# One stream for all attention tiles and feed-forward rounds of a six-layer block

## What is computed

```python
for i in range(6):
    x = attn_layer(shift_tokens(x), Wqkv[i], q_scale[i], k_scale[i], Wo[i]) + x
    x = ffn_layer(shift_tokens(x), ln_g[i], ln_b[i], W1[i], b1[i], W2[i], b2[i]) + x

def attn_layer(x, Wqkv, qs, ksc, Wo):        # 16 heads of 64
    q, k, v = split(x @ Wqkv)                # 128 -> 3 * 1024
    q = q / max(norm(q), 1e-12) * qs         # the floor under the norms
    k = k / max(norm(k), 1e-12) * ksc
    q, k = rotary(q), rotary(k)              # two products and a sum each
    out = local_attention(q, k, v)           # windows of 32, softmax
    return out @ Wo                          # 1024 -> 128

def ffn_layer(x, g, bln, W1, b1, W2, b2):
    xn = (x - mean) / sqrt(var + 1e-05) * g + bln
    a, gate = split(xn @ W1 + b1)            # 128 -> 2 * 341
    return a * gelu(gate) @ W2 + b2          # 341 -> 128
```

## Time and profile before

| | us |
|---|---|
| median of 3 runs | 4562.96 |
| lowest, highest | 4555.24, 4566.67 |
| the profiled execution | 4562.57 |
| its span on the core | 4560.5 |

### The profile page before, as it was taken

One profiled execution on the slowest core, in us unless ns is written; L12 is line 12 of the kernel. 1 busy time (PEld: TensorE's weight loads), 2 busy tenths in 40 slices (PEclk: granted clock), 3 DMA queues, 4 the chain that ended last, 5 costly groups with the idle time before them and its releaser, 6 DMA issues.

```text
span 4560.5 us, 148424 instructions
## 1 busy us (share of the span) xinstructions
PE 4214.2 (92%) x51751; PEld 2907.5 (64%) x51751; DVE 3501.8 (77%) x7368; ACT 2547.9 (56%) x5842; POOL 2884.7 (63%) x3664
## 2 busy tenths in 40 slices
PE   6999998999899988999889998999889998788899
PEld 4777775666666666666656666666666665566655
DVE  4666668997699967999679985999769995577566
ACT  2555555666466655666456663666546664355322
POOL 2333337887288855888378882888648885655300
PEclk9999999999999999999999998999999999887699
DMA  2000010000100010000100001000000000000000
GB/s 83 7 7 7 6 41 6 5 5 6 43 6 5 5 30 20 5 5 6 36 11 5 5 6 43 6 5 5 28 22 5 5 7 11 21 12 12 4 7 11
DMA packets 160438, 64.07 MB, mean 14 GB/s; under 512 B 121365, under 2 KB 155937, under 8 KB 159521
## 3 DMA queue, kind: packets, MB, share of 16 engines
q1 hardware_dynamic: 160288, 62.05, 5.3%
HBM read 26.54 MB, written 2.10 MB: 6 GB/s over the span
## 4 chain that ended last, share of the span: by engine, by line
PE 33%; DVE 29%; issue 25%; POOL 5%; ACT 4%; DVEq 1%; SPq 1%; ACTq 1%; POOLq 0%; DMA 0%
DVE ss L993 6%; DVE big L988 6%; DVE mx L1005 5%; PE pj L1535 3%; DVE big L987 3%; DVE e L1012 3%; DVE qn L987 3%; PE pj L1378 3%; PE turn L1454 3%; PE pp L1336 2%; PE sc L1547 2%; ACT big L698 2%; PE po L1351 2%; PE sc L1697 1%; PE turn L1535 1%
## 5 line engine op out<-in xcount | busy, mean ns | idle before, releaser
L1436 PE MATMUL pj<-wqkv,xcT 128*128 128x512 f32 x1536 | 830.4, 624 | 24.5 <-DVE big L988 9.6
L690 ACT ACTIVATE big<-pj 128x512 f32<-128x512 f32 x768 | 459.1, 598 | 244.3 <-PE pj L1436 176.1
L530 POOL TENSOR_TENSOR big<-big 128x512 f32<-128x512 f32 x384 | 486.0, 1277 | 132.0 <-DVE big L988 132.0
L988 DVE TENSOR_TENSOR big<-pj,ropes 128x512 f32<-128x512 f32 x768 | 522.4, 680 | 0.0
L530 POOL TENSOR_TENSOR qn<-qn,big 128x512 f32<-128x512 f32 x384 | 486.5, 1278 | 35.6 <-DVE big L988 35.6
L993 DVE TENSOR_REDUCE ss<-big 128x8 f32<-128x512 f32 x768 | 504.2, 678 | 0.1
L1524 PEld LDWEIGHTS pp<-wo,oT 128*128 128x128 f32 x3072 | 366.8, 196 | 154.5 <-ACT oT L713 154.1
L525 POOL TENSOR_TENSOR e<-e,rc 128x512 f32<-128x512 f32 x384 | 392.8, 1045 | 46.1 <-DVE rc L1023 46.1
L1524 PE MATMUL pp<-wo,oT 128*128 128x128 f32 x3072 | 403.9, 286 | 7.0 <-ACT oT L713 7.0
L519 POOL TENSOR_TENSOR qn<-qn,ny 128x512 f32<-128x512 f32 x384 | 396.9, 1045 | 7.5
L519 POOL TENSOR_TENSOR big<-big,ny 128x512 f32<-128x512 f32 x384 | 396.8, 1045 | 7.5
(11 more groups left out here) (322 smaller groups left out, 9605.8 us busy)
## 6 DMA issues: line engine op xcount, KB each, us to landing
wqkv<-in_L_ffn_Wqkv SPq DMA_DIRECT2D x6, 1536.0 KB, 6.5
xsd<-Y SPq DMA_DIRECT2D x192, 32.0 KB
xsd<-Y SPq DMA_DIRECT2D x384, 15.8 KB
xsf<-Y SPq DMA_DIRECT2D x96, 64.0 KB
xsf<-Y SPq DMA_DIRECT2D x192, 31.5 KB
xsx<-Y SPq DMA_DIRECT2D x64, 64.0 KB, 1.8
xsx<-CT SPq DMA_DIRECT2D x64, 64.0 KB, 1.9
wo<-in_L_ffn_Wo SPq DMA_DIRECT2D x6, 512.0 KB, 7.5
```

Of the source, the lines that this page charges most:

```text
L530: nc.gpsimd.tensor_tensor(U[a.par][i], U[a.par][i], t2b[i % 2], ALU.add).then_inc(sem("d_add"), 1)
L690: nc.scalar.activation(sqb[i % 2], pj[i % 2][:, :], ACT.Square).then_inc(sem("d_sq"), 1)
L988: nc.vector.tensor_tensor(t2v, swapped, sin, ALU.mult).then_inc(sem("d_r"), 1)
L1436: mm(pj[i % 2][:, :], xcT[:, a.par, :], wqkv[:, i * 512:i * 512 + 512], start=True, stop=True).then_inc(sem("d_ch"), 1)
```

## The change

The two phases of a layer and the six layers are one loop now. A `Pass` holds four tiles (stages `n`, `a`, `b`, `c`, as before) and five rounds (`rounds[0]` to `rounds[4]`, one stage each), and there is a pass for each of the 192 tiles and eight to drain. A round stage runs in every second pass: `hidden`, `gelu` and `gated` in the even ones (`even_round(3)`), statistics, normalisation and transposition (`odd_round(2)`) and the down projection with its residual sum (`odd_round(3)`) in the odd ones. Rounds trail the tiles by so much that their two tiles are finished. `all_layers` writes the first eight passes and the last eight out, and loops over the others: the eight passes at the seam of two layers once, the 24 inside a layer as six iterations of four.

What moves with it:

- `hidden` writes to `po[0]`, `po[1]`, `po[0]`, the banks of `pv`, and the GELU writes to a buffer of its own, `f_hidden`; `f_xcT` takes the place of `kT` as its input. The down projection writes to `pp` (before: `sc`) and the transpositions to `pt_` (before: `pp`).
- PE begins a pass with `chunk(0)` and not with `turn(0)`, and `turn` uses the banks `pt_` and `pp` in turn.
- ACT loads the GELU tables at the start of every even pass and the other set in the middle of it.
- On POOL `turn_sum(3)` stands ahead of the four small operations and of `unit(a, 0)`; `unit` and `probs` alternate.
- The weights are loaded in parts, each when its last reader is done: `wqkv` in three parts, `wo`, the norm, the up and the down weights. The eleven feed-forward loads stand between loads of tiles in SP's list.
- In the last layer the product with the gate, the sum into `X`, its statistics and its normalisation are spread over two passes, and the normalisation is on DVE (one `tensor_scalar` a tile) and not on POOL.
- `clamp` stays on DVE, ahead of `rope(3)`.

The core of the diff:

```diff
-        f_hid = [pj[0], pj[1], pt_]
+        f_hid = [po[0], po[1], po[0]]
+        f_hidden = sb("f_hidden", [P, 3, FT * P])
+        f_xcT = sb("f_xcT", [P, 2, FT * P])
...
+        LAGS, ROUND_LAGS, SEAM = 4, 5, 8
...
+        def all_layers(eng, body):
+            tiles, rounds = DEPTH * NT, DEPTH * NF
+            def known(k, **more):
...
+                body(Pass([one(k - i, tiles, NT) for i in range(LAGS)], [one(k // 2 - i, rounds, NF) for i in range(ROUND_LAGS)],
+                          k % 2, in_po=min(max(k - 3, 0), tiles), **more))
...
+            for k in range(SEAM):
+                known(k, at=k, layer=0)
+            with eng.Fori(0, DEPTH - 1) as l:
+                inside(l, False)
+                for p in range(SEAM):
+                    moving(l, NT + p, 0, at=p, layer=l + 1)
+            inside(DEPTH - 1, True)
+            for k in range(tiles, tiles + SEAM):
+                known(k, last=True)
...
+                if part == "q":
+                    past(sp, "d_ch", l * (4 * NT) - 2)
+                    sp.dma_start(wqkv[:, 0:INNER], Wqkv[l, :, 0:INNER]).then_inc(sem("wq_in"), 16)
...
+                unit(b, 1)
+                probs(0)
+                unit(b, 2)
+                probs(1)
+                unit(b, 3)
...
+                turn_sum(0)
+                mean_square(p.odd_round(2))
...
+                turn_sum(1)
+                inverse_deviation(p.odd_round(2))
...
+                turn_sum(2)
+                turn_sum(3)
...
+                if r:
+                    nc.scalar.preload_act_table_set("gelu_and_others")
+                square(0)
+                turned(0)
+                gelu(0)
...
+                if r or p.begins(0):
+                    nc.scalar.preload_act_table_set("natural_log_exp_and_others")
...
+                if p.begins(1):
+                    dve.wait_ge(sem("wq_in"), p.layer * 48 + 48)
...
+                rope(0)
+                square_sum(0)
+                gated(0)
+                rope(1)
+                if x:
+                    dve.wait_ge(sem("f_in%d" % x.par), x.half * 48 + 48)
+                    for i in range(FT):
+                        last = nc.vector.bn_stats(st[:, i, :], xsf[:, x.par, i, :])
...
+                clamp()
+                rope(3)
+                if x:
+                    past(dve, "f_rstd", x.g + 1)
+                    for i in range(FT):
+                        last = nc.vector.tensor_scalar(fxn[:, 128 * i:128 * i + 128], xsf[:, x.par, i, :], dif[:, 2 * i:2 * i + 1], rstd[:, i:i + 1], ALU.subtract, ALU.mult)
+                    last.then_inc(sem("f_xn"), 1)
+                if y:
+                    nc.vector.tensor_tensor(Y[:, ds, :], pp[:, 0:2 * D].rearrange("p (a d) -> p a d", a=2), Y[:, ds, :], ALU.add).then_inc(sem("y_ready"), FT)
                 row_max(0)
...
-                        for j in range(4):
-                            last = nc.tensor.transpose(pt_[:, j * P:j * P + P], U[b.par][i][:, j * P:j * P + P], ident)
+                        bank = (pt_, pp)[i % 2]
+                        for j in range(4):
+                            last = nc.tensor.transpose(bank[:, j * P:j * P + P], U[b.par][i][:, j * P:j * P + P], ident)
...
+                chunk(0)
+                hidden(0)
                 turn(0)
-                chunk(0)
                 turn(1)
                 chunk(1)
+                hidden(1)
```

More of the change, by code:

```diff
@@ L683, in _, with step @@
             stream(act, NT, x_body, 0, 0, 4)
[L685 removed]
+            def step(p):
+                n, a, b, c = p.n, p.a, p.b, p.c
+                r = p.even_round(3)
                 def square(i):
@@ L1121, in l_body @@
+            all_layers(dve, step)
             def l_body(a, b, c, d, e_, f):
@@ L1431, in chunk @@
                             past(pe, "d_xc", a.g + 1)
+                        if p.begins(1) and i % 2 == 0:
+                            pe.wait_ge(sem(("wq_in", "wk_in")[i // 2]), p.layer * (48, 32)[i // 2] + (48, 32)[i // 2])
                         if i < 2:
```

513 lines of the change are left out of this document (292 added, 221 removed).

## The result

| | us |
|---|---|
| kernel before, median (all its runs beside the changed one) | 4561.01 (4555.24 to 4566.67) |
| changed kernel, median | 4457.58 (4454.3 to 4462.36) |
| ratio | 0.9774, 95% interval 0.9757 to 0.9791 |
| profiled execution of the changed kernel; its span | 4454.3; 4452.4 |

The change makes the kernel 2.3% faster; 4441 was forecast. The spans of the two profiled executions differ by 108.1 us: 90.5 in the stretch of the layers, 15.2 in the last step (628.2 to 613.0 from its first transposition to the end), 2.4 ahead of the layers.

What follows compares the result with a forecast made beforehand. PE full and the loop through DVE closed bound a pass; filling and draining cost 40 us a layer. Pairs at 31.7 us, seams and ends gave 3113 us for the layers, 121 less: 4441 us, range 4345 to 4555.

Runs made afterwards that it cites:

- two_both: Changed kernel with two passes in its inner loop, the layers written out and all rotary tables worked out before the first layer; 4333.63 us, ratio 0.9497 to the kernel before.

## What to carry to other kernels

Count the instructions of a loop's body on its fullest engine before making it longer, and look at the instruction queue's packets and for idle time put down to "issue" at the loop's turn: here a body of four passes instead of two gave away 76 us of a possible 179. Where between 856 and 1699 instructions the edge lies, and what besides length sets it, these runs do not say. When phases are merged, write down the loop through each engine, POOL's too, because whichever order is changed for one waits in another. For a small DVE operation with both operands in SBUF, beside a busy POOL, the moment at which it starts sets its price: the same clamp costs 0.19, 0.77 or 1.04 us.

## What had not been expected of the hardware

- A turn of a loop whose 1699 PE instructions are read again costs 3.6 us of the stream, and 3.6 with twice the body (36.4 / 10); with 856 instructions it costs nothing. PE stands 2.0 to 2.4 us, and where its clock falls behind that, the turn costs 4.7 us and not 3.2.
- The same body in its second copy was read again at two of five turns only.
- Code that is run straight through cost nothing that could be seen: the five written-out seams of `two_both` add 1.4 us each, at 120 packets.
- An operand addressed through a register in the eight rotary products of a pass cost 0.12 us a pair.
- 0.6 us more on an engine cost 1.37 us a pair, since it moved the next instruction out of a gap of POOL.
